# An EdgeConv layer with a sorted-segment maximum: where the final rows are fetched, and where the chain's steps stand

## What is computed

```python
def _L0_gnn_ref(x, W, b, edge_index):
    src, dst = (edge_index[0], edge_index[1])
    x_i = x[dst]
    x_j = x[src]
    feat = jnp.concatenate([x_i, x_j - x_i], axis=-1)
    msg = feat @ W.T + b
    out = jax.ops.segment_max(msg, dst, num_segments=x.shape[0])
    return jnp.where(jnp.isfinite(out), out, 0.0)
h = jnp.maximum(_layernorm(x, axis=-1), 0.0)
x = x + _L0_gnn_ref(h, L0_gnn_W, L0_gnn_b, edge_index)
```

## Time and profile before

| | us |
|---|---|
| median of 3 runs | 991.62 |
| lowest and highest | 990.52, 994.15 |
| the profiled execution | 995.42 |
| its span, first to last instruction | 993.8 |
| PE, DVE, ACT, POOL busy | 564.1, 846.5, 577.9, 713.8 |
| granted TensorE clock, mean | 0.825 of full |

### The profile page before, as it was taken

The page is one execution under the profiler, slowest core; times in us unless marked ns, Lnnn a source line. Parts: engine busy times, 40 slices in busy tenths (PEclk is TensorE's granted clock), DMA queues, the critical chain, the costliest instruction groups (busy, mean ns, idle before and its releaser), DMA issues.

```text
span 993.8 us, 7917 instructions
## 1 busy us (share of the span) xinstructions
PE 564.1 (57%) x2393; PEld 265.1 (27%) x2393; DVE 846.5 (85%) x1237; ACT 577.9 (58%) x255; POOL 713.8 (72%) x644
## 2 busy tenths in 40 slices
PE   2556970000002366766776676788878888676560
PEld 2443640000001122322222232333333333222240
DVE  7899899987785598999989999899999999758573
ACT  3775113000038999597996987496797976844000
POOL 1587878888875677677767676676777677777745
PEclk9898995555555779888878987999999999988875
DMA  8831222212146466656657776998988778754344
GB/s 256 194 97 21 70 71 79 67 50 77 55 145 217 142 208 223 197 174 222 179 170 232 255 253 201 295 296 300 338 302 321 278 239 259 227 186 139 73 79 148
DMA packets 62901, 182.11 MB, mean 183 GB/s; under 512 B 20358, under 2 KB 33140, under 8 KB 56315
## 3 DMA queue, kind: packets, MB, share of 16 engines
q1 hardware_dynamic: 42530, 140.13, 40.7%
q0 software_dynamic: 20144, 40.52, 17.1%
q10 hardware_dynamic: 184, 0.96, 0.3%
HBM read 127.34 MB, written 55.04 MB: 184 GB/s over the span
## 4 chain that ended last, share of the span: by engine, by line
POOL 29%; DVE 26%; issue 19%; DMA 13%; PE 8%; ACT 3%; POOLq 0%; DVEq 0%; SPq 0%; PEldq 0%
POOL rows L669 22%; DVE acc L1191 10%; DMA rows<-near_table,idx 8%; PE ps L787 8%; DVE maxima L1134 5%; POOL ohs L641 4%; POOL hT L648 3%; DVE hT L1141 3%; DMA running_max<-maxima 2%; DVE pos L878 2%; DVE hT L1154 1%; DVE ohs L1179 1%; DMA ohs<-in_dst,begin_i 1%; DMA ohs<-winners 1%; DVE hT L1146 1%
## 5 line engine op out<-in xcount | busy, mean ns | idle before, releaser
L669 POOL DMA_INDIRECT rows<-near_table,idx x527 | 600.3, 1139 | 206.0 <-issue 138.8
L787 PE MATMUL ps<-ohs,near 128*128 128x481 bf16 x1443 | 351.9, 401 | 142.6 <-DVE acc L1191 119.7
L1191 DVE TENSOR_TENSOR acc<-ps,acc 128x1924 f32<-128x1924 f32 x192 | 336.5, 1779 | 21.8 <-PE ps L787 21.6
L1134 DVE SCALAR_TENSOR_TENSOR maxima<-maxima,fresh,rows 128x128 f32<-128x128 f32 x527 | 185.6, 352 | 72.6 <-DMA rows<-near_table,idx 56.2
L787 PEld LDWEIGHTS ps<-ohs,near 128*128 128x128 bf16 x1443 | 143.7, 105 | 350.1 <-DVE acc L1191 125.8
L548 ACT ACTIVATE ohs<-ohs,neg_l 128x6272 bf16<-128x6272 bf16 x25 | 137.9, 5518 | 123.4 <-DMA ohs<-winners 123.4
L541 ACT ACTIVATE hT<-k,off 128x2400 bf16<-128x2400 int16 x49 | 108.9, 2281 | 131.7 <-DVE hT L1146 115.6
L550 ACT ACTIVATE ohs<-ohs 128x6272 bf16<-128x6272 bf16 x25 | 135.8, 5431 | 0.8
L787 PE MATMUL ps<-sorts_mem,near 128*128 128x481 bf16 x468 | 107.8, 385 | 32.7 <-DVE acc L1191 28.6
L773 PE MATMUL ps<-flags,ones 128*128 128x8 f32 x2 | 0.6, 356 | 173.0 <-DVE spare L1167 173.0
L641 POOL DMA_INDIRECT ohs<-src_pad,start_i x49 | 55.0, 1122 | 34.9 <-DVE start_i L891 20.5
(11 more groups left out here) (173 smaller groups left out, 517.4 us busy)
## 6 DMA issues: line engine op xcount, KB each, us to landing
ohs<-winners SPq DMA_DIRECT2D x37, 1568.0 KB, 7.7
running_max<-maxima SPq DMA_DIRECT2D x90, 512.0 KB, 5.1
sorts_mem<-winners SPq DMA_DIRECT2D x12, 1568.0 KB, 8.0
rows<-near_table,idx POOLq DMA_INDIRECT x527
acc<-in_x SPq DMA_DIRECT2D x6, 512.0 KB, 8.2
near_table<-acc SPq DMA_DIRECT2D x12, 256.0 KB, 4.5
base<-in_x SPq DMA_DIRECT2D x1, 2744.0 KB
out_x<-hT SPq DMA_DIRECT2D x12, 224.0 KB
```

The source lines that it names most:

```text
L669: nc.gpsimd.indirect_dma_start(rows[:, n % (SLOTS * GATHERS), :], None, near_table[:, :], bass.IndirectOffsetOnAxis(idx[:, n:n + 1], 0)).t ...
L787: last = nc.tensor.matmul(bank(4 * (n % 2) + c - UNITS[r][0])[:, 0:CHUNK], near[:, t, part, :], oh[t % OHS][:, at:at + CHUNK], start=part ...
L1134: V.scalar_tensor_tensor(run_at(n + 1), run_at(n), fresh[:, n:n + 1], rows[:, n % (SLOTS * GATHERS), :], ALU.add, ALU.max).then_inc(chain, 1)
L1191: V.tensor_tensor(into, found, into, ALU.max).then_inc(max_done, 1)
```

## The change

Three edits go together.

- **Three homes.** The running maxima are kept in three tables: steps 0 to 415 for columns 0 to 35, 232 to 503 for columns 36 to 43, 296 to 527 for columns 44 to 48. Blocks of eight steps from 296 to 415 are stored three times. SP issues 117 stores in place of 90. Two flags more are computed and checked (a range in which a column's end must lie).
- **Finals.** POOL issues all 527 gathers without a break, then 36 finals, then the test of `disorder` and `decided`, then 8 finals and 5 finals. POOL's six additions (L692) are gone: DVE adds all 13 groups, each directly behind its join.
- **Order.** `schedule()` assumes gathers of 1.45, 2.0 and 1.28 us by phase (before 1.85 and 1.3) and a cost of 3.65 for the round beside DVE's one-hot.

```diff
-CUT, CUT_CAP, CUT_LOW = 36, 416, 232
-FINALS_FROM, FINALS_EVERY = 448, 8
+HOMES = ((0, 36, 0, 416), (36, 44, 232, 504), (44, 49, 296, 528))
+EARLY = HOMES[0][1] // GROUP
...
-        pieces += [("round", 1.85)] * 4
+        pieces += [("round", 1.85)] * 2 + [("round", 3.65 if t % 4 == 0 else 1.85)] + [("round", 1.85)]
...
+    phase, gather = "lists", {"lists": 1.45, "words": 2.0, "round": 1.28}
...
-                issue += GATHERS * (1.3 if name == "round" else 1.85)
+                issue += GATHERS * gather[phase]
...
-            return [(0, n)] * (n < CUT_CAP) + [(1, 0)] * (n == 0) + [(1, n - CUT_LOW + STEPS)] * (n >= CUT_LOW)
+            return [(h, n - low + STEPS * (low > 0) if n else 0) for h, (_, _, low, cap) in enumerate(HOMES)
+                    if n == 0 or low <= n < cap]
...
-                for g in range(early_groups):
-                    if (b + 1) * GATHERS == FINALS_FROM + g * FINALS_EVERY:
-                        if g == 0:
-                            pool.wait_ge(m_ready, len(batches))
-                            stored(CUT_CAP // STEPS)
-                        finals(g)
-
+
+            pool.wait_ge(m_ready, len(batches))
+            stored(HOMES[0][3] // STEPS)
+            for g in range(EARLY):
+                finals(g)
             pool.wait_ge(disorder_ready, 1)
...
             pool.sem_inc(decided, 1)
-            stored(all_blocks)
-            for g in range(early_groups, groups):
+            for g in range(EARLY, groups):
+                for home in HOMES[1:]:
+                    if spans[g][0] == home[0]:
+                        stored(home[3] // STEPS)
                 finals(g)
-            for g, (a, z) in enumerate(spans):
-                if by_pool(g):
-                    pool.wait_ge(joined, g + 1)
-                    nc.gpsimd.tensor_tensor(rowsF[:, a:z, :], rowsF[:, a:z, :], base[:, a:z, :], ALU.add).then_inc(final_added, 1)
...
-                if not by_pool(g):
-                    dve.wait_ge(joined, g + 1)
-                    V.tensor_tensor(rowsF[:, a:z, :], rowsF[:, a:z, :], base[:, a:z, :], ALU.add).then_inc(final_ready, 1)
+                dve.wait_ge(joined, g + 1)
+                V.tensor_tensor(rowsF[:, a:z, :], rowsF[:, a:z, :], base[:, a:z, :], ALU.add).then_inc(final_ready, 1)
```

More of the change, by code:

```diff
@@ L96, in schedule @@
         here = []
+        if name in gather:
+            phase = name
         if name == "list":
@@ L646, in finals @@
                 for j in range(a, z):
-                    h = 0 if j < CUT else 1
+                    h = sum(j >= end for _, end, _, _ in HOMES)
                     nc.gpsimd.indirect_dma_start(
```

39 lines of the change are left out of this document (19 added, 20 removed).

## The result

The changed kernel is slower: 1019.56 us (1015.95 to 1021.88, 4 runs) against 992.54 (990.52 to 994.15, 4 runs) of the kernel before on the same chip, a ratio of 1.0265 (95%: 1.0237 to 1.0292). The forecast was 992.5 with a range of 978 to 1008.

The account below looks back on a forecast made before the run. Neither POOL nor DVE was taken to bound alone; POOL's gathers pace the chain, then the rounds, then the tail. Chain's end 898.8 + rounds 74.5 + tail 21.4 = 994.7 us of span, 992.5 us as median; range 978 to 1008.

Parts of the forecast that it names:

- What bounds the kernel: Neither POOL nor DVE alone: POOL waits for DVE's full slots up to 850 us, then DVE waits 30.6 us for gathers.
- The landings, 3 us: POOL's gathers: the 27 extra stores add 3 us to its waits for landings, between bounds of 0 and 39 us.
- The rival: Slower by landings: threefold stores delay POOL's gathers, as a batch awaits the one two before; 19 us, 1009 us; chance 0.22.
- The finals, 45.0 us: POOL: 36 finals of 1.25 us leave the stretch of gathers, so the last gather ends 45.0 us earlier.
- - 22.0 (waits for DVE): POOL between 340 and 952 us: its 22.0 us of real waits for full slots go, but for 2 us left in.
- Landing of the last batch, 2.5 us: Behind the last gather: landing takes 2.5 us and the last bundle 1.5, so the chain ends at 898.8 us.
- The front, 12.5 us: Ahead of the rounds: two more bundles before tree 1 shift the first round by 12.5 us, to 349.3.
- 33 rounds, 74.5 us: Behind the chain's end: 33 rounds without steps, 9.11 us a tile by the PE and DVE handover, take 74.5 us.
- Tail 21.4 us: Last round to the span's end: 21.4 us in place of 40.7, with all of POOL's additions gone.
- The clock rival: Slower: PE's clock falls after idling and stays so in 8 tiles, 52 us more, 1044 us; chance 0.05.
- The port: POOL's gathers slowed by DVE instructions holding a shared port: fewer gathers or finals beside them don't reduce it; left in the sum.

Follow-up runs that it names:

- e2: The changed kernel with two tables of running maxima in place of three, finals and order as changed: 1131.0 us, 1.0268 of the kernel before.
- k2: The changed kernel with two tables, assumed gather costs 1.85 then 1.38 us, each four finals waiting for the previous four to land: 989.46 us, 0.9942 of the kernel before.
- k1: The kernel before with DVE making all 13 additions and POOL none: 984.97 us, 0.9906 of the kernel before.
- e4: The changed kernel with the assumed gather costs ahead of the first round set back to 1.85 us: 1128.51 us, 1.0233 of the kernel before.
- h1: The kernel before with only the changed order of steps (the new assumed costs in `schedule()`): 1144.77 us, 1.0562 of the kernel before.
- f4: The changed kernel with assumed gather costs of 1.85 us ahead of the rounds and 1.38 in them: 1093.1 us, 0.991 of the kernel before.
- e3: The changed kernel with the order of steps of the kernel before (its assumed costs): 1073.08 us, 0.9776 of the kernel before.
- g3: The changed kernel with one batch of gathers under way (`FLYING = 1`) in place of two: 1425.47 us, 1.298 of the kernel before.
- h4: The changed kernel with the old order, two tables, and each four finals waiting until the four before have landed: 1046.77 us, 0.9627 of the kernel before.
- f3: The changed kernel with the order of steps of the kernel before, run again on another chip: 1075.6 us, 0.9768 of the kernel before.
- g4: The changed kernel with the old order, each four finals waiting until the four before have landed: 1061.68 us, 0.9724 of the kernel before.

## Why the prediction was wrong, step by step

- **What bounds the kernel: half right.** POOL's waits for full slots were real, 20.1 us by the landing records for the 22.0 taken from the names, all of them ahead of gather 360. That the waits for landings would hold POOL in their place was left to 3 us.
- **The landings, 3 us: the step that failed.** The sum kept the waits for landings at what they had been and added 3 us for the 27 stores. They grew by 28.7 us, from 17.6 to 46.3. Of the 19.5 us by which the last gather is late, 25.7 are this and 1.6 the front, less 9.5 of shorter gathers (below); 1.7 us are left over. The rival named the right wait ("POOL may not issue a batch until the one two before has landed") and was given 0.22, up to 1009; but it had the extra stores as its cause, and e2 shows no loss by them under this order, on its kind of chip.
- **The finals, 45.0 us: right as a count, not as a gain.** No final is left among the gathers. But while the finals stood there the landings had time: the last 79 gathers needed 101.0 us beside the finals and 117.3 without, 16.3 of the 45 back, nearly all of it (15.7) in waits for landings, which no run with the finals between has there. This is the larger half of the step that failed: the finals' time was taken off as if nothing else went on in it.
- **"- 22.0 (waits for DVE)": came in.** The waits for slots went from 20.1 us to none, and gathers 112 to 359, where all of them had been, took 21.0 us less. In these, 7.0 us went to waits for landings, and the gathers themselves got 7.9 us shorter; that the two cancel is luck. Gathers 360 to 447 took 5.6 us more, with 6.0 more of waits for landings.
- **The whole stretch.** From gather 112 to the end of the last gather it was 951.8 - 313.3 = 638.5 us before, so 593.5 without 45 us of finals; after, it was 914.3 - 319.9 = 594.4. That these agree to 1 us is a coincidence of the parts above (21.0 less, then 5.6 and 16.3 more), not a fixed pace. k2 needed 906.5 - 314.4 = 592.1, and k1, with the order of before, 946.3 - 314.0 - 45.0 = 587.3.
- **Landing of the last batch, 2.5 us: 7.3.** With 1.5 for the bundle, 4.0 became 8.5 us. Together with the last gather's 19.5 us this is the 24 us at the chain's end.
- **The front, 12.5 us: 9.7**, list 6.6 us later as forecast near 5. e4, which takes this back, ends no earlier: right that the front as such isn't the end.
- **33 rounds, 74.5 us: 74.4.** The argument from one tile, that a tile costs 9.1 us by the handover however few steps are in it, held: 9.04. (The 7.4 us for DVE alone, 2.07 + 3 x 1.57 + 0.46, add up to 7.24; nothing in the sum hangs on it.) This is also why emptying the last tiles brings so little: 7.5 tiles at 9.1 us remain whatever was moved out of them.
- **Tail 21.4 us: 20.1**, its gain of 20 us as worked out.
- **The clock rival: in a few tiles only.** Mean granted clock 0.820 against 0.825, and the last tiles run at full pace (18 matmuls in 3.86 us, as in the earlier trace rows). Where DVE stood at a bundle, PE stood too, and its next matmuls were slower, as here in the timeline of PE after, at 828.82, 18 in 6.68 us:

```profile
828.82 6.68 PE L778 MATMUL ps<-sorts_mem,near 128*128 128x481 bf16 x18 [6.86 <-DVE acc L1188]
```

PE's busy time grew by 5.7 us in all, not by 52. The Trainium skill's rule ("TensorE: Matmul & The Clock Gate", "What's actually happening") agrees with both: slower behind idle time, full pace in the last rounds, which have short waits only.
- **The port**: POOL's gathers still take up to 2.4 us where the shortest take 0.94; gathers' time over 0.944 us from the 112th on was 38.1 us before, 28.6 after. So the part that the sum left in became 9.5 us less, and without that the waits for landings would have shown in full.

What the order did to DVE is the other half. The sum took the chain's end as POOL's alone and asked nothing of what DVE does meanwhile. With 12 steps a tile up to tile 20, at 1.43 us a gather, DVE meets bundles that aren't there (the 42.4 us above) while rounds which it could do stand behind them. Those rounds are then left for the end, at 9 us a tile. h1 shows this part alone, on a chip with standstills, and f4 shows how steep it is: 0.10 us a gather in the assumption moved the result by 3%.

**Open.** How much of the loss on a chip like the first is the order and how much the moved finals: the runs that take one of them alone (e3, h1) all ran on chips with standstills, and there POOL's waits are partly others. What a third batch under way would be worth on a chip without standstills: not run there. What the standstill is: only that it comes with POOL's unbroken issuing, in g3 within one run, and that gaps take away much of it; by what way POOL's issuing would stop PE and DVE was not found. Why some chips show it and others don't. h4 was run only on a chip that shows it, and k1 together with h4's placing of finals nowhere.

## What to carry to other kernels

Work that stands between transfers may be giving them the time to land: before its time is booked as a gain, work out from the trace what the transfers' own wait would be without it (here 16 of 45 us came back). Where an instruction waits for two semaphores, look how far the second one is behind when the first is taken away, and count instructions issued against done rather than trust the releaser's name. When a static order interleaves two streams, place the pieces of the slower stream by the pace measured with all its waits (here 1.43 us a gather), not by the issue time (1.25): being early stops everything queued behind (42.4 us of DVE here), being late fills the slots (20.1 us of POOL before). And a stage with a floor by handover (9.05 us a tile) gains nothing from being emptied further; k1, a change of the tail alone, got 9 us.

## What the runs showed of the hardware

- Chips differ: on four of them the same kernel took 1085 to 1101 us in place of 992 to 994, with the durations of DVE's rounds, of gathers and of packets unchanged, PE's mean clock at 0.802 in place of 0.825, and with standstills of PE and DVE of up to 20 us, which the profile puts down to "remote" or "issue", while POOL issues indirect DMAs every 1.25 us and up to 6 us beyond. In g3 they came to 43.4 us beside 49 finals without a gap, and to none beside gathers of which one batch of four was under way at a time.
- After, a gather's landing was 2.4 us at the least, 3.4 in the median from 353 to 650 us and 5.9 from 650 to 850 us, 9.3 at the most, with the DMA queues 80.8% busy (65.7% and 15.1%, 640 to 700 us), less than the 88% of the earlier trace rows. Over the last 79 gathers a batch landed in 4.2 us in the mean with finals between (4.5 in k1) and in 6.6 without (6.1 in k2).
- POOL started its next batch 0.76 us behind the last landing that it had waited for, and 0.27 us behind the step of DVE that freed its slots.
- Gaps of some 1.7 to 2.4 us after every four finals brought the time from the last gather to the chain's last step from 80 us (f3) to 28 us (g4) on two such chips, and cost 17.9 us of POOL's time on one without standstills.
